# Three of four roundings of the exponentials moved from VectorE to GpSimd in the last attention layer

## What is computed

```python
q = _fq_sym(transpose(q * scale), axis=-1); k = _fq_sym(transpose(k), axis=-1); v = _fq_sym(v, axis=2)
attn = jnp.einsum('bhqd,bhkd->bhqk', q, k)
attn = jax.nn.softmax(attn.astype(jnp.float32), axis=-1)
attn = _fq_unsigned(attn, axis=-1)       # s = max(attn)/255;  q = clip(round(attn/s), 0, 255)*s
out = jnp.einsum('bhqk,bhkd->bhqd', attn, v)
return out @ Wp + bp                     # then x = x + tanh(gate) * this
```

## Time and profile before

| what | value |
|---|---|
| median of 3 runs | 3354.78 us (3352.99 to 3357.09) |
| profiled execution, first to last instruction | 3349.9 us |
| around the span, against the median | 4.9 us |
| busy in the span | PE 85%, DVE 64%, ACT 47%, POOL 11% |
| the loop of this layer, first to last exponential | 2426 to 2921 us |

### The profile page before, as it was taken

One profiled execution on the slowest core, in us unless ns is written; L12 is line 12 of the kernel. 1 busy time (PEld: TensorE's weight loads), 2 busy tenths in 40 slices (PEclk: granted clock), 3 DMA queues, 4 the chain that ended last, 5 costly groups with the idle time before them and its releaser, 6 DMA issues. The chain is left out here.

```text
span 3349.9 us, 46674 instructions
## 1 busy us (share of the span) xinstructions
PE 2832.3 (85%) x15008; PEld 1835.0 (55%) x15010; DVE 2142.2 (64%) x5173; ACT 1559.7 (47%) x3247; POOL 376.7 (11%) x675
## 2 busy tenths in 40 slices
PE   7888995898899999638999999836599999857898
PEld 4334664777677777515777777624222223234676
DVE  5675337777666666574444444578999999677432
ACT  4452225888767777452222222213266666624221
POOL 0010004322322212010000000040300000002100
PEclk9798997999999999958999999877699999977899
DMA  1002003000000000003000000001000000020000
GB/s 57 1 2 86 0 4 123 14 1 14 14 8 1 7 1 1 23 11 126 1 1 1 0 0 0 19 5 40 0 1 1 1 1 1 1 96 2 1 0 13
DMA packets 37907, 56.93 MB, mean 17 GB/s; under 512 B 6400, under 2 KB 25792, under 8 KB 36416
## 3 DMA queue, kind: packets, MB, share of 16 engines
q1 hardware_dynamic: 37696, 54.35, 4.8%
HBM read 52.99 MB, written 1.05 MB: 16 GB/s over the span
## 5 line engine op out<-in xcount | busy, mean ns | idle before, releaser
L2754 ACT ACTIVATE a_exps<-psum,a_ln 128x512 f32<-128x512 f32 x512 | 315.0, 684 | 191.0 <-PE psum L2684 191.0
L2825 DVE TENSOR_REDUCE a_half_max<-psum 128x1 f32<-128x1024 f32 x256 | 311.3, 1219 | 12.5 <-PE psum L2667 5.9
L1902 DVE TENSOR_REDUCE a_neg_max<-psum 128x2 f32<-128x512 f32 (+1 forms) x128 | 122.5, 957 | 174.6 <-PE psum L1597 171.8
L1617 PE MATMUL psum<-a_probs_t,a_vals 128*128 128x256 f32 x768 | 192.0, 386 | 18.2 <-ACT a_probs_t L1774 18.1
L2684 PE MATMUL psum<-a_qs,a_ks 99*128 99x512 bf16 x512 | 173.6, 389 | 34.6 <-ACT a_exps L2754 22.8
L847 DVE SCALAR_TENSOR_TENSOR f_silu<-f_silu,psum 128x352 f32<-128x352 f32 (+2 forms) x88 | 50.4, 573 | 229.8 <-ACT f_silu L820 229.7
L1097 DVE TENSOR_REDUCE a_neg_max<-psum 128x2 f32<-128x1024 f32 x64 | 78.4, 1225 | 177.2 <-PE psum L1092 177.2
L1597 PE MATMUL psum<-a_k_t,a_q_t 128*128 128x256 f32 (+1 forms) x512 | 190.7, 496 | 0.9 <-ACT a_probs L1782 0.9
L1742 ACT ACTIVATE a_normed<-psum,a_head_bias,a_head_scale 128x128 f32<-128x128 f32 x448 | 169.4, 466 | 41.0 <-POOL a_head_bias L1561 40.7
L2869 DVE TENSOR_SCALAR a_probs<-a_exps 128x1024 bf16<-128x1024 f32 x256 | 175.1, 685 | 14.5 <-ACT a_exps L2754 14.5
L1556 POOL TENSOR_TENSOR a_head_rstd<-a_head_var,neg_half 128x4 f32<-128x4 f32 x112 | 113.9, 1017 | 596.4 <-DVE a_head_var L1896 410.9
(11 more groups left out here) (480 smaller groups left out, 6118.9 us busy)
## 6 DMA issues: line engine op xcount, KB each, us to landing
a_w_raw<-in_L_xattn_wproj_dram SPq DMA_DIRECT2D x8, 512.0 KB, 3.8
f_w_silu<-in_L_ffn_gate_dram SPq DMA_DIRECT2D x1, 2112.0 KB, 9.7
f_w_mul<-in_L_ffn_up_dram SPq DMA_DIRECT2D x1, 2112.0 KB, 14.3
a_probs<-in_ctx_t_dram SPq DMA_DIRECT2D x4, 512.0 KB, 5.1
f_w_silu<-in_L_ffn_Wu_dram SPq DMA_DIRECT2D x1, 2048.0 KB, 7.8
f_w_mul<-in_L_ffn_Wg_dram SPq DMA_DIRECT2D x1, 2048.0 KB, 12.5
f_w_down<-in_L_ffn_Wd_dram SPq DMA_DIRECT2D x1, 2048.0 KB, 17.7
a_q_raw<-in_L_xattn_wq_dram SPq DMA_DIRECT2D x4, 512.0 KB, 6.9
```

The costliest lines, as they stand in the source:

```text
L1617: mm = pe.matmul(core.bank(OUT)[:, 0:S], vals[:, quad % 2, j, (h // 2) * P:(h // 2 + 1) * P], probs_t[:, g % 2, j, :], start=(j == 0), sto ...
L2754: act.activation(exps[:, n % UNITS, :], core.bank(LOGITS + u), ACT.Exp, bias=ln255[:, :]).then_inc(exp_ready, 1)
L2825: v.tensor_reduce(half_max[:, h, t, half:half + 1], ring(("scores", s)), AX.X, ALU.max, negate=True).then_inc(ring_free, 1)
```

## The change

Pairs with m % 4 == 3 are still rounded on the DVE, by the same instruction. The other three of four are rounded on POOL, in two instructions: (x * 1.0 + ROUND) into an fp32 tile `lifted`, a wait for it, and then (that - ROUND) * 1.0 into bf16 `probs`. `lifted` is two tiles deep and lies in `xn_t`; `probs` grows from four pairs to six and lies in `stack_ones`; both are idle in the loop. `exps` grows from 12 tiles to 16. `group` comes two slots later (lag 5 instead of 3), and so do `keep_out`, `turn_heads` and `keep_heads`: the last two move from slots 1 and 9 of 16 to slots 3 and 11. There are two semaphores more.

```diff
-        UNITS, PAIRS, TILES_PER = 12, 4, 4
+        UNITS, PAIRS, TILES_PER = 16, 6, 4
         exps = sb("exps", [P, UNITS, QC])
-        probs = sb("probs", [P, PAIRS, 2 * QC], BF16)
+        probs = stack_ones[:, :, :, :].rearrange("p t h c -> p (t h c)")[:, 0:PAIRS * 2 * QC].rearrange("p (u n) -> p u n", u=PAIRS)
+        lifted = xn_t
...
+        GROUP_LAG = 5
-        SLOT_COUNT = LAG + H * PER + 8
+        SLOT_COUNT = LAG + H * PER + 8 + GROUP_LAG - 3
...
-            g, k = divmod(s - LAG - 3, 2)
+            g, k = divmod(s - LAG - GROUP_LAG, 2)
...
+        def by_vector(m):
+            return m % 4 == 3
...
-            n, k = divmod(s - LAG - 2 * GROUPS - lag, 2 * GROUPS)
+            n, k = divmod(s - LAG - 2 * GROUPS - (GROUP_LAG - 3) - lag, 2 * GROUPS)
...
             @block.gpsimd
+                for m in range(H * PER):
+                    if by_vector(m):
+                        continue
+                    done, first = rounded_by_pool(m), 2 * m % UNITS
+                    up = lifted[:, done % 2, :]
+                    g.wait_ge(exp_ready, 2 * m + 2)
+                    g.tensor_scalar(up, exps[:, first:first + 2, :].rearrange("p u n -> p (u n)"), 1.0, ROUND, ALU.mult, ALU.add).then_inc(lifted_ready, 1)
+                    at_least(g, weighted_done, (m - PAIRS) // 2 + 1)
+                    g.wait_ge(lifted_ready, done + 1)
+                    g.tensor_scalar(probs[:, m % PAIRS, :], up, -ROUND, 1.0, ALU.add, ALU.mult).then_inc(probs_by_pool, 1)
...
-                    pe.wait_ge(probs_ready, 2 * (g + 1))
+                    at_least(pe, probs_by_pool, rounded_by_pool(2 * (g + 1)))
+                    at_least(pe, probs_by_vector, rounded_by_vector(2 * (g + 1)))
...
-                    if pair_at(s - 1) is not None:
+                    if pair_at(s - 1) is not None and by_vector(pair_at(s - 1)):
                         round_pair(pair_at(s - 1))
```

More of the change, by code:

```diff
@@ L2509, in layer3_attention @@
         shifted, rstd = sb("shifted", [P, NT]), sb("rstd", [P, NT])
-        UNITS, PAIRS, TILES_PER = 12, 4, 4
+        UNITS, PAIRS, TILES_PER = 16, 6, 4
         exps = sb("exps", [P, UNITS, QC])
-        ctx_t = exps[:, 2 * B:UNITS, :].rearrange("p (r k) n -> p r k n", k=DK)
+        ctx_t = exps[:, 2 * B:2 * B + 2 * DK, :].rearrange("p (r k) n -> p r k n", k=DK)
         head_in = sb("head_in", [P, 2, 2, D])
@@ L2537, in layer3_attention @@
         rows_kept, rows_in0, rows_in1 = sem("rows_kept"), sem("rows_in0"), sem("rows_in1")
-        logits_full, exp_ready, probs_ready, weighted_done = sem("logits_full"), sem("exp_ready"), sem("probs_ready"), sem("weighted_done")
+        logits_full, exp_ready, weighted_done = sem("logits_full"), sem("exp_ready"), sem("weighted_done")
+        probs_by_pool, probs_by_vector, lifted_ready = sem("probs_by_pool"), sem("probs_by_vector"), sem("lifted_ready")
         out_kept, turned_full, heads_kept = sem("out_kept"), sem("turned_full"), sem("heads_kept")
@@ L2569, in group_at, with rounded_by_vector, rounded_by_pool @@
         def group_at(s):
-            g, k = divmod(s - LAG - 3, 2)
+            g, k = divmod(s - LAG - GROUP_LAG, 2)
             return g if k == 0 and 0 <= g < CHUNKS * GROUPS else None
+        def by_vector(m):
+            return m % 4 == 3
+        def rounded_by_vector(m):
+            return sum(by_vector(k) for k in range(m))
+        def rounded_by_pool(m):
+            return m - rounded_by_vector(m)
         def chunk_at(s, lag):
-            n, k = divmod(s - LAG - 2 * GROUPS - lag, 2 * GROUPS)
+            n, k = divmod(s - LAG - 2 * GROUPS - (GROUP_LAG - 3) - lag, 2 * GROUPS)
             return n if k == 0 and 0 <= n < CHUNKS else None
@@ L2869, in round_pair @@
                     v.tensor_scalar(probs[:, m % PAIRS, :], exps[:, first:first + 2, :].rearrange("p u n -> p (u n)"),
-                                    ROUND, ROUND, ALU.add, ALU.subtract).then_inc(probs_ready, 1)
+                                    ROUND, ROUND, ALU.add, ALU.subtract).then_inc(probs_by_vector, 1)
                 for s in range(SLOT_COUNT):
```

## The result

| | before | after |
|---|---|---|
| median of 4 runs each, one chip | 3355.08 us (3352.99 to 3357.09) | 3390.93 us (3386.89 to 3395.49) |
| span of the profiled execution | 3349.9 us | 3388.0 us |
| mean granted clock of PE | 0.924 | 0.918 |

The changed kernel is slower: ratio 1.0116, 95% interval 1.0104 to 1.0128. The predicted time, 3394, is 3 us away. Two of its terms were wrong, though, and they nearly cancel, so the closeness is partly luck. In part 2 one run of the kernel without POOL's roundings took 3920.08 us at a mean granted clock of 0.722 and is left out of its figures.

What follows compares the result with a forecast made beforehand. The PE and ACT chain, not the DVE, bounds regular slots. Per head 3.23 + 0.15 - 0.96 = +2.42 us, +36 over fifteen splits, +3 at the loop's end: span 3388.9, plus 4.9 around it, 3394 us; range 3338 to 3430.

Steps and rivals of the forecast that it cites:

- The chain, and what a faster DVE can bring: PE and ACT, without DVE, keep two regular slots at 3.70 us; a faster DVE brings at most 23 us.
- The split into 0.62 and 0.34: Around the split: 0.62 us a head from earlier B maxima, 0.34 from moving `turn_heads` away; possible gain 0.96.
- POOL's instruction, 1.04 us: Each POOL rounding instruction of 1024 elements takes 1.04 us, the time of a copy of 128x1024.
- Three whole waits, 3.23 us: At the split, the first DVE instruction waits 0.11, the next three 1.04 each for POOL, the fifth none: 3.23 us.
- The 0.15 us for a late B slot: After the split's step, a late B slot costs perhaps 0.15 us more, since slot 17's maxima free the ring.
- The other waits, counted as 0: The DVE's one rounding in four and the two-input instruction of `keep_heads` wait up to 1.04 us for POOL; counted as 0.
- The clock should stay at the upper level: PE's clock in the loop stays at 2.4 GHz, with PE near 85% busy; falling in the stalls would be wrong.
- The 4.9 us "around the span": Time outside the span, 4.9 us, added to the predicted span of 3388.9 us to give 3393.8.
- POOL's +3: In the loop's last 21 slots POOL needs 7.4 us for four slots where the chain has 6.54: +3 us.
- Waits absent: Rival: the split's waits are absent or fall where POOL idles; 15 us faster, 3340 us; chance 0.13.
- POOL the bound: Rival: with quick instructions POOL needs above 7.40 us in four slots and its backlog grows; beyond 3430, chance 0.08.
- A slow form: Rival: one or both POOL instructions cost 3.43 ns an element, so POOL bounds the loop; 3790 or 4264, chance 0.12.

Runs made afterwards that it cites:

- part 2: Series with its own runs of the kernel before (median 3353.45 us): all roundings on DVE 3357.48, none on POOL 3331.98, single-instruction POOL rounding 3562.77.
- the best version: Changed kernel with POOL held back during the split and the last 21 pairs rounded on the DVE: 3336.00 us, ratio 0.9948 against the kernel before.
- the second edit: Changed kernel with POOL held one instruction later, ahead of the next pair, so one more runs beside the split: 3348.11 us, ratio 0.9991 against the kernel before.
- the third edit: Changed kernel with the last 21 pairs all rounded on the DVE: 3383.36 us, ratio 1.0107 against the kernel before.

## Why the prediction was right, and where it was not

**The chain, and what a faster DVE can bring: right.** Regular steps stay at 3.70 to 3.71 us (2502.85 to 2506.56 after). Taking all of POOL's roundings out left heads of 30.30, a gain of 0.89 us where I had 0.96. The whole gain was 20 us, against at most 23.

**The split into 0.62 and 0.34: the second was wrongly explained.** I gave 0.34 us to the move of `turn_heads`. With all roundings on the DVE the move cost 0.14 us a head (31.33), and taking them off the DVE then gave 1.03 (30.30). That the sum came near 0.96 is luck in the parts. A relieved DVE without the move was not run.

**POOL's instruction, 1.04 us: right**, with 1.08 and 1.05 on average. The distance between the two dependent instructions is 0.15 us, not the 0.08 to 0.09 that I took.

**Three whole waits, 3.23 us: the mechanism right, the size too large, the count right by luck.** The step over the split was to take 7.26 us and took 6.19. The times of the second, third and fifth instruction are 0.90, 0.92 and 0.88 us, so the waits are 0.73, 0.75 and 0.71, 2.19 together. Each of the three begins 0.14 to 0.18 us after POOL's instruction has begun and ends 0.02 to 0.03 us after it, so it takes about 1.04 - 0.16 + 0.02 = 0.90 us, its own 0.17 in it. I had charged the full 1.04 on top of 0.17. I also had the fourth wait and the fifth go through, with POOL out of work; in fact POOL still works, the fourth slips through the 0.15 us between its dependent instructions, and the fifth waits. The 0.15 us for a late B slot did not come: where the clock stays up the next step takes 3.71 us.

The Trainium skill's "SBUF — State Buffer", "Who interferes with whom", calls the shared port pair an exclusive lock. The three waits that end with POOL's instruction agree, to 0.03 us in the rows shown, and so do the five times of 0.17 us with POOL held back. The Trainium skill's section has the other engine blocked for the whole instruction. The slow (add, subtract) does not agree: the wait beside it ended 1.05 us into an instruction of 3.62, and for this form the measurement decides.

**The other waits, counted as 0: right.** The last instruction of `keep_heads`, 0.23 us before, takes 0.93 on average, and the rounding left on the DVE takes 0.69 as before. The regular steps stay at 3.70.

**"The clock should stay at the upper level": wrong.** This is the step that failed, and the prediction named it as a sign of being wrong. I argued from PE's busy share over a whole head, near 85%. Twelve of fourteen heads met the granted clock of 0.50 behind the stall, eleven of them for about 3.4 us, at 1.41 us a head on average and 1.49 where the steps can be compared. With eight idle matmuls in the stall it did not fall once in the loop. A busy share over a long stretch does not say it: in the best version's tail PE is busy 30.86 of 37.37 us, 83%, at a granted clock of 1.00. What decides when it falls stays open. The two heads that were spared have the same stall of 2.17 us as the others, and two heads of the kernel before met the lower level with a stall of 0.20 us. In single traces the count of such heads is 2 of 14 with a stall of 0.20 us at `rows` (before), 5 with 0.62, 3 with 0.71 (the second edit) and 12 with 2.18.

The Trainium skill's "TensorE: Matmul & The Clock Gate" says in "Part 1: The HAM clock gate" that the gated state is the default and that activity releases it. The kernel with filler matmuls agrees, with 1.00 over 474 us where the changed kernel had 0.95.

**The sum.** Predicted +2.42 us a head: -0.96 + 3.23 + 0.15. Measured +2.35: -0.89 of relief, +2.11 of waits, +1.41 of the lower level, and 0.28 less because four of the fourteen heads before were longer too, two of them at the lower level. The waits were taken 1.27 too large, with the late B slot in them, and the clock's 1.41 is missing. That these two cancel is luck, and that is why the total looks better than its parts.

**The 4.9 us "around the span": two things in one.** In the changed kernel's profiled execution time and span differ by 2.0 us (3389.99 and 3388.0), and in no execution on record by more. So the other 3 us of the 4.9 must be that the profiled execution before was quicker than the median of its runs. The span came out at 3388.0 against the 3388.9 predicted.

**The tail: POOL's +3 right, the clock missing again.** Fifteen splits were priced at 2.42, fourteen in the heads and one, the last, in the tail, so the tail was to grow by 5.4 us and grew by 8.6. The tails of the kernels give the parts, each from one trace: 36.4 before; 37.2 with every rounding on the DVE, so the later group and the deeper buffers cost 0.8; 40.1 with POOL held back at the splits, so its roundings cost 2.9; 40.8 with the waits back and filler matmuls, at the upper level throughout, so the waits cost 0.7; 45.0 in the changed kernel, so the 13.7 us at a clock of 0.51 cost 4.2. Taken in another order the parts differ: beside the low clock POOL's are worth 1.2 (the third edit).

In the other direction, the start gave back 5.3 us that were not foreseen. 2.9 of them lie ahead of the first split, and are no more than executions differ by: the first split begins anywhere from 2400.9 to 2407.2 in the kernels here with roundings on POOL. The first head took 36.4 to 36.9 us in each kernel with quick roundings on POOL, and 38.0 to 39.3 in those without, the one with no rounding there at all among them (38.35). The cause was not tested.

**The rivals.** *Waits absent* (3340, a ratio of 0.9955) was not this kernel, but holding POOL back nearly made it, at 0.9963; that its time reads 3340.09 is chance, since the kernel before is quicker in that series. *POOL the bound* falls: it idles 109.6 us before the exponentials. *A slow form* is real for (add, subtract), and was not used.

## What to carry to other kernels

Before work moves to GpSimd, list the small VectorE instructions on SBUF that lie on the critical path, and lay GpSimd's queue beside them: each can wait until GpSimd's instruction is over, however small it is itself (0.71 to 0.75 us beside 1.04 here, 3.43 beside 3.60 before the loop), and one semaphore wait that keeps GpSimd out for 1.4 us recovered all of it here (1.0116 to 0.9963, and 0.9948 with the tail on VectorE). A busy share of 96% was no bound: 132 us off the VectorE were worth 20. A stall of PE costs more than its length if the clock falls behind it, so look at the granted clock of the step after the stall, and try idle matmuls in the stall.

## What the runs showed of the hardware that was not expected

- A stall of PE of 2.2 us in a head of 32.4 was followed by 3.4 us at the lower clock in eleven of fourteen heads and by 6.8 us in one; after the last split it was 13.7 us. Eight filler matmuls, which raised PE's busy time in the split's step from 3.70 to 5.44 us, removed it from the loop.
- GpSimd's tensor_scalar on 128x1024 takes 1.04 us as (mult, add) in fp32 and as (add, mult) to bf16, and 3.71 us as (add, subtract) to bf16 (one run, 192 instructions). The pair of operations sets the time.
- Beside a (add, subtract) instruction of 3.62 us a 128x8 instruction of VectorE waited only until that was 1.05 us old. Its group in that kernel's loop has a mean of 0.92 us.
- Between two dependent GpSimd instructions 0.15 us pass, enough for one 128x8 instruction of VectorE to slip through; between independent ones (2509.15, after 2508.14 + 1.04) none pass.
